# Eight projection rounds for the last attention, moved from the first layer of a fused transformer kernel to the end of its sixth

## The reference, cut to what matters

```
k = (encoder_hidden_states @ Wk).reshape(B, Skv, H, D)
v = (encoder_hidden_states @ Wv).reshape(B, Skv, H, D)
k = rmsnorm(k, gk)
```

## Time and profile before

| | |
|---|---|
| median of 3 runs | 1470.12 us (1469.28 to 1470.72) |
| the profiled execution's own time | 1469.43 us |
| its span, first to last instruction | 1467.7 us |
| mean granted TensorE clock | 0.945 |
| PE busy | 1312.8 us, 89% |
| DVE busy | 1046.7 us, 71% |
| ACT busy | 721.2 us, 49% |
| POOL busy | 216.6 us, 15% |
| chain that ended last | PE 69%, DVE 10%, ACT 3%, issue 2%, DMA 1% |

### The profile page before, as it was taken

The page is one execution under the profiler, slowest core; times in us unless marked ns, Lnnn a source line. Parts: engine busy times, 40 slices in busy tenths (PEclk is TensorE's granted clock), DMA queues, the critical chain, the costliest instruction groups (busy, mean ns, idle before and its releaser), DMA issues.

```text
span 1467.7 us, 21005 instructions
## 1 busy us (share of the span) xinstructions
PE 1312.8 (89%) x6692; PEld 919.3 (63%) x6701; DVE 1046.7 (71%) x2211; ACT 721.2 (49%) x1836; POOL 216.6 (15%) x227
## 2 busy tenths in 40 slices
PE   8788869989999658999999799994999999989998
PEld 4344445555334335677767589993888888765555
DVE  7999977888996796877788723235666666667665
ACT  5788823342776574655455212223666666633111
POOL 0122220000000001212221074111111111201000
PEclk9899969999999769999999789997999999989999
DMA  5122250006430200000103199854322222101330
GB/s 191 72 100 91 96 193 1 0 15 103 63 61 4 83 0 1 1 9 29 37 1 106 35 345 329 303 208 158 119 71 71 71 71 71 36 1 48 78 93 29
DMA packets 77777, 124.62 MB, mean 85 GB/s; under 512 B 44965, under 2 KB 56430, under 8 KB 72352
## 3 DMA queue, kind: packets, MB, share of 16 engines
q1 hardware_dynamic: 75824, 119.37, 25.5%
q0 software_dynamic: 1872, 4.22, 0.8%
HBM read 88.28 MB, written 26.24 MB: 78 GB/s over the span
## 4 chain that ended last, share of the span: by engine, by line
PE 69%; DVE 10%; ACT 3%; issue 2%; DMA 1%; POOL 0%; SPq 0%; DVEq 0%; ACTq 0%; POOLq 0%
PE psum L2411 6%; PE psum L3210 5%; PE psum L1983 4%; PE psum L2759 4%; PE psum L873 4%; PE psum L2707 4%; PE psum L2737 4%; PE psum L2025 4%; PE psum L2772 3%; PE psum L3220 3%; PE psum L2422 3%; DVE roomB L1539 2%; PE psum L2015 2%; PE psum L2715 2%; PE psum L907 2%
## 5 line engine op out<-in xcount | busy, mean ns | idle before, releaser
L2829 ACT ACTIVATE roomA<-psum,roomA 128x256 f32<-128x256 f32 x128 | 71.0, 559 | 87.1 <-DVE roomA L2896 86.7
L2080 ACT ACTIVATE roomA<-psum,roomA 128x128 f32<-128x128 f32 (+1 forms) x128 | 53.4, 427 | 84.3 <-DVE roomA L2155 84.1
L1539 DVE TENSOR_REDUCE roomB<-psum 128x2 f32<-128x512 f32 x128 | 81.5, 686 | 10.3 <-PE psum L1378 9.6
L2559 DVE SCALAR_TENSOR_TENSOR roomA<-roomA,psum 128x512 f32<-128x512 f32 x23 | 15.9, 690 | 95.6 <-ACT roomA L2458 89.4
L753 DVE TENSOR_TENSOR_SCAN roomA<-roomA 128x1024 f32<-128x1024 f32 x32 | 78.8, 2463 | 0.0
L1983 PE MATMUL psum<-own,roomB 128*128 128x512 f32 x160 | 75.0, 594 | 3.5 <-DVE roomA L2147 2.1
L1946 POOL TENSOR_TENSOR roomA<-roomA 128x512 f32<-128x512 f32 x40 | 51.0, 1277 | 176.8 <-DVE roomA L2148 176.8
L3210 PE MATMUL psum<-roomA,roomB 128*112 128x512 f32 (+1 forms) x168 | 74.8, 593 | 0.3 <-DVE roomA L3438 0.3
L2759 PE MATMUL psum<-roomA 128*128 128x256 f32 x256 | 67.5, 386 | 1.8 <-ACT roomA L2837 0.7
L2737 PE MATMUL psum<-roomA 128*128 128x256 f32 x256 | 65.6, 379 | 1.7 <-ACT roomA L2829 1.7
L3318 ACT ACTIVATE roomA<-psum 48x512 f32<-48x512 f32 (+1 forms) x32 | 19.0, 594 | 97.8 <-PE psum L3210 97.8
(11 more groups left out here) (519 smaller groups left out, 3372.7 us busy)
## 6 DMA issues: line engine op xcount, KB each, us to landing
roomB<-m_w_dram SPq DMA_DIRECT2D x12, 1536.0 KB
roomA<-m_w_dram SPq DMA_DIRECT2D x11, 1536.0 KB
a_kv_ready<-roomB SPq DMA_DIRECT2D x32, 512.0 KB, 3.1
roomA<-a_kv_ready SPq DMA_DIRECT2D x8, 1024.0 KB, 4.9
roomA<-a_kv_ready SPq DMA_DIRECT2D x16, 512.0 KB, 4.2
roomB<-a_w_dram SPq DMA_DIRECT2D x4, 1280.0 KB, 5.6
roomB<-f_w_dram SPq DMA_DIRECT2D x8, 624.0 KB, 3.8
roomA<-f_c_rows SPq DMA_DIRECT2D x6, 512.0 KB, 4.0
```

The lines of the kernel that those rows point to most:

```text
L1539: dve.tensor_reduce(maxneg[:, hp // 8, :, m, hp % 8], g.bank(m).rearrange("p (q k) -> p q k", k=S), AX.X, ALU.max, negate=True).then_inc(s ...
```

## The change

The last eight rounds are taken out of `mamba`: there are now 24 rounds in it, eight before the loop (values, as before) and one in each iteration, always keys. The last round of the loop now being keys, its `squares` follow it on ACT. SP waits for the squares at the end of its list.

In `moe3` the eight value rounds of the last four head pairs are added. Their weights (`v_late`, 512 KB) are loaded on SP's queue with the small inputs of the layer, whose semaphore now counts 64. After the last down projection PE does eight rounds, alternately into banks 4 and 5 and into banks 6 and 7. From the third on, each waits for ACT's copy of the round two before. ACT, after its last copy of a down projection, copies each round to a staging buffer, waits for that copy, and issues the store of 512 KB from its own queue. From the fifth round on its copy first waits for stores: the fifth and sixth for the stores of the first and second, the seventh and eighth for those of the third and fourth. The staging buffers are three pieces of a tile that the layer has done with, and one free piece. The seventh layer's SP list waits for all these stores before its loop.

Some one-off semaphores of `moe3` are merged, which changes no order that matters.

```
@@ mamba
-    EARLY, MIDDLE, EXTRA = 5, 3, (0, 2, 4, 6, 8, 10, 12, 14)
+    EARLY, MIDDLE = 5, 3
...
-        in_loop[n] = [EARLY + MIDDLE + n + sum(e < n for e in EXTRA) + k for k in range(1 + (n in EXTRA))]
-    assert in_loop[-1][-1] == 31
-    values = list(range(EARLY + MIDDLE)) + [in_loop[n][0] for n in EXTRA[0:7]] + [31]
+        in_loop[n] = [EARLY + MIDDLE + n]
+    ROUNDS = 32 - LATE_V
+    assert in_loop[-1][-1] == ROUNDS - 1
+    values = list(range(EARLY + MIDDLE))
...
         for k in range(4):
-            sp.wait_ge(s[f"m_kv_stored{k}"], 8 * 16)
+            sp.wait_ge(s[f"m_kv_stored{k}"], ROUNDS // 4 * 16)
+        sp.wait_ge(s["m_k_squared"], 16)
...
-        pe.wait_ge(s["m_kv_copied"], 32)
+        pe.wait_ge(s["m_kv_copied"], ROUNDS)
...
         kv_out(in_loop[-1][-1])
+        squares(in_loop[-1][-1])
@@ moe3
+LATE_V = 8
...
+    v_late = kept.take(LATE_V // 2, 2 * P)
+    spare = Room(room.tensor, room.size)
+    spare.at = 17600
+    v_staged = hot.rearrange("p h i n -> p (h i n)").rearrange("p (k q t) -> p k q t", k=3, q=2)
+    v_staged = [v_staged[:, k] for k in range(3)] + [spare.take(2, HALF)]
+    v_stored = lambda r: s[f"m3_v_stored{min(r // 2, 2)}"]
...
-        sp.dma_start(steps_of, d["m3_steps"]).then_inc(s["m3_steps"], 16)
+        sp.dma_start(steps_of, d["m3_steps"]).then_inc(s["m3_small"], 16)
+        sp.dma_start(v_late, d["a4_kv"].rearrange("p (n k) c -> p n k c", k=2)[:, 8 - LATE_V // 2:, 1]).then_inc(s["m3_small"], 16)
...
+        def late_values(r):
+            if r < 2:
+                pe.wait_ge(s["m3_h"], NB)
+            else:
+                pe.wait_ge(s["m3_y"], NB + r - 1)
+            for i in range(4):
+                t = 4 * (r % 2) + i
+                ins = pe.matmul(g.ps[:, (4 + 2 * (r % 2)) * HALF + i * 2 * P:(4 + 2 * (r % 2)) * HALF + (i + 1) * 2 * P],
+                                g.CT[:, t * P:(t + 1) * P], v_late[:, r // 2, :], start=True, stop=True)
+            ins.then_inc(s["m3_up"], 1)
...
+        for r in range(LATE_V):
+            late_values(r)
...
+        late_values_out(act)
+
+    def late_values_out(act):
+        for r in range(LATE_V):
+            act.wait_ge(s["m3_up"], NB + r + 1)
+            if r >= 4:
+                act.wait_ge(v_stored(r - 4), 32)
+            src = g.ps[:, (4 + 2 * (r % 2)) * HALF:(6 + 2 * (r % 2)) * HALF].rearrange("p (i q c) -> p q i c", i=4, q=2)
+            act.copy(v_staged[r % 4].rearrange("p q (i c) -> p q i c", i=4), src).then_inc(s["m3_y"], 1)
+            act.wait_ge(s["m3_y"], NB + r + 1)
+            act.dma_start(g.kv[8 - LATE_V // 2 + r // 2, 1, :, :, r % 2 * HALF:(r % 2 + 1) * HALF], v_staged[r % 4])\
+               .then_inc(v_stored(r), 16)
@@ attn4
         g.f5_first(sp)
+        for k in range(3):
+            sp.wait_ge(s[f"m3_v_stored{k}"], 16 * (2, 2, LATE_V - 4)[k])
```

More of the change, by code:

```diff
@@ L456, in mamba @@
     for n in range(NS):
-        in_loop[n] = [EARLY + MIDDLE + n + sum(e < n for e in EXTRA) + k for k in range(1 + (n in EXTRA))]
-    assert in_loop[-1][-1] == 31
-    values = list(range(EARLY + MIDDLE)) + [in_loop[n][0] for n in EXTRA[0:7]] + [31]
-    keys = [r for r in range(32) if r not in values]
-    kind_of = [int(r in values) for r in range(32)]
-    place_of = [(values if kind_of[r] else keys).index(r) for r in range(32)]
+        in_loop[n] = [EARLY + MIDDLE + n]
+    ROUNDS = 32 - LATE_V
+    assert in_loop[-1][-1] == ROUNDS - 1
+    values = list(range(EARLY + MIDDLE))
+    keys = [r for r in range(ROUNDS) if r not in values]
+    kind_of = [int(r in values) for r in range(ROUNDS)]
+    place_of = [(values if kind_of[r] else keys).index(r) for r in range(ROUNDS)]
     xpad = ra.take(E2, B, S + TAPS - 1)
@@ L481, in sync @@
         sp.dma_start(w_kv[:, 4:16], d["a4_kv"][:, 4:16]).then_inc(s["m_kv_in"], 16)
-        for r in range(32):
+        for r in range(ROUNDS):
             sp.wait_ge(s["m_kv_copied"], r + 1)
@@ L2340, in gpsimd @@
     def gpsimd(pool):
[L2341 to L2345, removed]
+        pool.memset(none[:, 0:D + 2], 0.0).then_inc(s["m3_set"], 1)
+        pool.memset(none[:, D + 2:], 4.0 * TOK).then_inc(s["m3_set"], 1)
+        pool.memset(ones, 1.0).then_inc(s["m3_set"], 1)
+        pool.memset(first, 1.0).then_inc(s["m3_set"], 1)
+        pool.wait_ge(s["m3_set"], 4)
         pool.affine_select(out=first, in_=first, compare_op=ALU.is_gt, fill=0.0, base=0,
-                           pattern=[[1, P]], channel_multiplier=-1).then_inc(s["m3_first"], 1)
+                           pattern=[[1, P]], channel_multiplier=-1).then_inc(s["m3_set"], 1)
         pool.wait_ge(s["m3_cleared"], 16)
@@ L2373, in tensor @@
         logits(pe, 1)
-        pe.wait_ge(s["m3_first"], 2)
-        pe.wait_ge(s["m3_ones"], 1)
+        pe.wait_ge(s["m3_set"], 5)
         pe.wait_ge(s["m3_mask"], 2)
@@ L2577, in moe3 @@
     g.done_count += 1
-    head = norm_halves(g, src=g.XN, dst=tok[:, :, 0:D], rms=True, gain=gain, gain_in=(s["m3_small"], 32), between=lambda pe: logits(pe, 0), meanwhile=(lambda dve: ranks(dve, 0), lambda dve: ranked(dve, 0)))
+    head = norm_halves(g, src=g.XN, dst=tok[:, :, 0:D], rms=True, gain=gain, gain_in=(s["m3_small"], 64), between=lambda pe: logits(pe, 0), meanwhile=(lambda dve: ranks(dve, 0), lambda dve: ranked(dve, 0)))
     xt_done = g.xt_done
-    early = dict(sync=sync, gpsimd=gpsimd, scalar=lambda act: act.wait_ge(s["m3_small"], 32))
+    early = dict(sync=sync, gpsimd=gpsimd, scalar=lambda act: act.wait_ge(s["m3_small"], 64))
     g.last_adds = [lambda dve, i=i: add(dve, i) for i in range(NT)]
```

8 lines of the change are left out of this document (4 added, 4 removed).

## The result

The change makes the kernel slower by 0.44%. The median after is 1475.22 us (six runs, 1473.09 to 1477.81), beside 1470.17 us for the kernel before in the same rounds (six runs, 1468.82 to 1471.14). The ratio is 1.0044, with a 95% interval of 1.0026 to 1.0062, so 5.05 us.

A forecast was written before the change was run, and what follows sets the result against it. DVE was taken to bound the loop, transfers and DVE the tail. The terms 0 + 1.4 + 0 + 0 + 3.4 gave +4.8 us, forecast 1474.5 us, range 1469.6 to 1478.3.

The forecast's parts named there:

- Rounds in the loop: State-space loop: eight rounds leaving it gain 0 us, since DVE is busy 8.24 of 8.45 us per iteration either way.
- The loop's start: First loop iteration: with one round fewer PE's clock rises later, delaying DVE by 1.4 us, bounds 0 to 2.6.
- Squares, the load of v_late, merged waits: After the last loop round and in the sparse layer's inputs: covered by slack before first use, 0 us.
- The stores beside the loads: Sparse layer's tail: eight stores share the DMA engines with eight loads, making the second transposes 3.4 us late.
- the engines take pieces in turn: DMA engines in the tail: alternating between both queues' pieces, a load goes at 2.26 us instead of 0.82.
- The term of the second half: Tail, second half: the eighth load lands 4.6 us late for DVE, of which 3.0 arrive at the second transposes.
- the third rival: Tail: engines share by bytes, a load takes 1.54 us, ACT's queue ends last, L241 4.5 us late; 1473.8 us, chance 0.17.
- the first keys' load meet none of the stores: After the tail: stores are over at about 1012 us, the first keys' load is issued at about 1013.
- PE's clock in the tail: Tail: PE's added work might keep its clock high, up to -1.4 us; given no weight in the sum.
- Nothing interferes: Rival, tail: loads and stores overlap and the clock stays high, with the loop's start at 0; 1468.8 us, chance 0.13.
- Only orders and clocks: Rival: loads not late, ACT's 1.4 us at L241 arrives whole, or only the loop's start costs; 1472.0 us, chance 0.20.
- The rounds in the loop did cost: Rival, loop: removing eight rounds wins at most 1.0 us each; 1462 to 1467 us with the tail, chance 0.05.

The follow-up runs named there:

- loop_only: Kernel after without any rounds in the sparse layer's tail, late values copied DRAM to DRAM instead; 1470.68 us, ratio 1.0011 to the kernel before.
- before_warm_tail: Kernel before plus nine groups of four unread matmuls on TensorE after the last down projection; 1468.87 us, ratio 0.9999 to the kernel before.
- warm_loop: Kernel after plus four unread matmuls on TensorE in the state-space loop's first iteration; 1475.87 us, ratio 1.0046 to the kernel before.
- seven_buffers: Kernel after with seven staging buffers instead of four, so only the eighth copy waits for a store; 1471.89 us, ratio 1.0018 to the kernel before.
- tail_four: Kernel before's loop with all 32 rounds, plus only four rounds run and stored in the tail; 1470.38 us, ratio 1.0011 to the kernel before.
- sp_eight: Kernel after with eight staging buffers and the eight stores issued by SP behind the eight loads; 1468.46 us, ratio 0.9997 to the kernel before.
- sp_stores: Kernel after with seven staging buffers and the eight stores issued by SP behind the eight loads; 1472.95 us, ratio 1.0027 to the kernel before.
- tail_no_stores: Kernel before's loop with all 32 rounds, plus the eight tail rounds computed and copied but not stored; 1469.73 us, ratio 1.0002 to the kernel before.

## Why the prediction was right, point by point

**Rounds in the loop: 0 predicted, 0 measured.** 8.45 us for an iteration with either number of rounds; loop_only is not faster than before.

**The loop's start: 1.4 us predicted; 0.7 in the profile of the change, 0.5 to 1.9 over five profiles.** In the profiles the mechanism is the one named, and the size lies within the bounds of 0 to 2.6. In the profile of the change the term measures half of what I put. PE began at 52.21 us, the add ran at half speed as worked out, and the round came at 59.80. I had the clock rise at 60.3; it rose at about 59.5. In kernels whose first iteration has two rounds the wait came up too, once with 0.52 us (before_warm_tail), and warm_loop gave no time back. So the size is not shown beyond these profiles.

**Squares, the load of v_late, merged waits: 0.** SP's next issue behind the loop is at 195.98 us, 1.15 us later than in the earlier trace rows, and that is the 0.7 us of the loop's start and the 0.4 by which x landed later. loop_only, which has the squares last too, lost 1.6 us, and its wait at the loop's start alone is 1.93.

**The stores beside the loads: 3.4 us predicted, 4.35 measured to the second transposes.** That the sum came near was luck: the loads' lateness was put too high and ACT's waits too low, and the loop's start, put 0.7 us too high, made up for most of the 0.95 us missing here. The step that I chose, that the engines take pieces in turn so that a load takes 2.26 us, failed: it takes 1.39, and 1.54 was the figure by bytes. My 0.82 us for a load alone was a share of busy time, not a spacing; by their landings the loads before were 0.99 us apart. At 356 GB/s the window from 992 to 1003 us moved 3.9 MB, while between six and seven loads (1.6 to 1.8 MB) landed, so a little over half was stores. The fourth load was 1.6 us late, not 3.9, counted at DVE's add (999.73 - 985.97 = 13.76 us beside 12.20 before). The term of the second half failed with it: the eighth load was to be 4.6 us late for DVE, and DVE's add of it came at 1007.60 - 985.97 = 21.63 us beside 20.08, 1.55 us late, without a wait for that load. In its place ACT's queue ended last, as the third rival said: waits of 1.88 and 3.06 us for stores, L241 4.7 us later (rival: 4.5), and at the slow clock all of it arrives, less 0.4 us. So the number of the forecast stood near the measured one, but the mechanism of the tail was the rival's, which should have had the greater chance. seven_buffers and tail_four show both parts apart, sp_eight shows both gone. The prediction also had the first keys' load meet none of the stores. It was issued at 1008.67 us, before the last store had landed at 1009.4, and cost nothing there.

**The rule of the Trainium skill**, "DMA: Bandwidth & Descriptors", "Issuing engines are not separate DMA queues": the trace agrees, in that the first load on SP's queue went from 2.67 to 4.2 us with stores on ScalarE's, and was back at 2.6 us in sp_stores. On the time for issues this trace has a loss beside the gain: SP's eight issues took 7.39 us instead of 3.96.

**PE's clock in the tail: weight 0 predicted, 0 found.** It fell at about 1005 us, after PE had stood idle from 1002.5, and L304 took 1.97 us as before. before_warm_tail prices the matter at 1.4 us where nothing else is late, as in the prediction, and shows most of it given back after the next pauses.

**The other rivals.** "Nothing interferes" fell with the first load's landing. "Only orders and clocks" had its 1.4 us at L241 about right: with the issues, which tail_no_stores lacks, ACT is through 1.3 us late in seven_buffers. It fell because the loads were late and ACT waited for stores. How much of such a 1.3 us would reach the second transposes no run shows; of the 0.57 us in tail_no_stores 0.2 did. "The rounds in the loop did cost" fell with loop_only.

## What to carry to other kernels

An idle stretch of one engine is only free for work whose transfers and whose place in every in-order queue are free as well: here 16 idle us on TensorE and ScalarE took eight rounds at no cost that could be measured, and their stores cost 4 to 5 us. When a buffer is used again, count the landing time under the load that will be there, not the one measured alone (3.1 us became up to 7.5), and look at who stands behind the waiting copy. Count each buffer's store by itself, so that a copy doesn't wait for a store whose buffer it does not use (read from the landings, not tried here). If such work must go there, queue its stores behind the loads that the critical path waits for, and give it a buffer for each store in flight.

## What the runs showed of the hardware

- Stores of 2 KB pieces on ScalarE's queue beside loads of 1 KB pieces on SyncE's moved 407 GB/s at a DMA share of 1.07, where the loads alone gave 275 GB/s at 0.87. The second queue isn't needed for it: sp_eight issues all stores from SyncE and moves as much (columns as in the earlier trace rows). The share is no fixed rate.

```profile
1003.00:1006.50 3.50, 1.09 (x8) 0.86 (x8) 3.33 (x9) 2.75 (x6) 0.00 (x0) 1.00 1.05 406
```

- Adding up the times alone still came near for the total: 18 us were predicted for all loads and stores, and the last store (issued at 1006.19, landing 3.2 us later) was there at 1009.4 us, 17.6 us after the first store's data could start, 1.1 us behind its issue at 990.67. What came out otherwise was who got the engines in between.
- SP's issue of a 256 KB load took 812 ns in the median and up to 1608 ns beside ScalarE's stores (469 in the median before); the eight issues took 7.39 us instead of 3.96. A second queue isn't needed for this either: in sp_eight SP's issue of a 512 KB store took 1206 ns in the median, beside 533 in the loop. The issuing engine itself is slowed.
- ScalarE's issue of a 512 KB store takes 542 ns of its own in-order list, as SP's does.
- After the loop's start the clock rose at anything from 56.7 to 61.1 us in profiles of kernels with the same or nearly the same start. In the tail, L304 after the same idle time of 3.07 us ran at 1.2 GHz in tail_no_stores and at 2.4 GHz in sp_eight. One profile of such a stretch is no measurement of its price.
